# W product and scaling two tiles later, and each rstd broadcast as one transfer to 128 partitions

## The chip, the cores and the metric

The kernel runs on one core of one Trainium2 chip. The metric is device time in microseconds (us): the median over the runs of one kernel.

## The reference

The input x is float32 of shape (2, 64, 256, 256): two images, 64 channels, 65,536 positions each. Four residual steps follow one another:

```python
x = x + conv3x3_depthwise(ln_c(x))                 # layer norm over the 64 channels, eps 1e-6
t = t + scan(batchnorm(ln_t(t) @ W.T), V)          # t: x as tokens; y = sigmoid(wx_t + y @ V.T) along the tokens
x = x + linear_attention(ln_c(x))                  # queries from every position, keys from every 4th row and column
t = t + experts(ln_t(t))                           # 32 experts, each takes its 8 best tokens of the 65,536
```

Each layer norm is (v - mean) / sqrt(var + eps) over the 64 channels of one position. So each position of each image needs one number, rstd = 1 / sqrt(var + eps), and all 64 channels of that position are multiplied by it.

## The kernel before

**Layout.** The 128 partitions hold image times channel: partitions 0 to 63 are the channels of image 0, partitions 64 to 127 those of image 1. The positions lie along the free axis. A tile is 512 positions (128x512, 128 tiles), a block is four tiles (128x2048, 1 MB, 32 blocks). Mean subtraction and the sums over channels are TensorE products with small constant matrices.

**How rstd reaches the channels.** The statistics of a block come out as one rstd number per image and position, on 4 partitions per image (512 positions each). SyncE (SP) writes them to a DRAM scratch, 8 KB per image (`rstd_to_dram`, line 350: one transfer per image, 4 rows of 2 KB). Then it reads each image's row of 2048 numbers back into 64 partitions at once (`rstd_to_channels`, line 359, and line 1313 in the attention stage), which makes a 128x2048 tile that VectorE multiplies with. That is two transfers of 512 KB for each block and norm. For the first norm the tile is `rb[0]`, for the second `rb[1]` (both shown as rstd_wide), for the attention stage `rb3` (rstd_of_channels). Each has two slots, so block k uses slot k % 2.

**The first stage (lines 214 to 635)** computes the first residual step and, behind it, the second norm and the W product. It is a software pipeline written by hand: each engine runs a Python loop over steps t, one tile per step, and each operation of tile g stands at step g + lag. The lags are in one line:

```python
SQ, CENTER, TAPS, SUMS, FINISH, SQ1, PROJECT, SCALE = -4, 5, 8, 9, 10, 12, 20, 21
STATS = (0, 16)
```

In words: ScalarE squares x at g - 4; TensorE sums block n's statistics at step 4n (`stats_of`, for block n of the first norm and block n - 4 of the second in one round n); VectorE forms the variance at 4n + 1 (line 605); ScalarE turns it into rstd at 4n + 2; TensorE centers tile g at g + 5 and VectorE multiplies it by rstd (`norm_x`, line 576); the nine taps of the convolution are shared out between TensorE (line 431), VectorE (line 599) and ScalarE with GpSimd (lines 509 and 541); GpSimd finishes x1 at g + 10 (line 548); TensorE makes the W product at g + 20 (`project`, line 446) and VectorE scales it by the second rstd at g + 21 (`scale_wx`, line 614), into `u`, a ring of two blocks shown as wx. On VectorE, at one step, the order is: first tap, `scale_wx`, second tap, variance, other taps, `norm_x`.

SP is a queue of its own, in program order. For each step t it does, as far as they fall due: the rstd writes of round n at t = 4n + 2, the broadcasts of round n at 4n + 3 (first norm of block n, then second norm of block n - 4), `store_x1` of block k at 4k + 14 (line 366), `store_u` of block k at 4k + SCALE + 4 = 4k + 25 (line 370), and the load of block k of x at 4k - 7 (line 344). Every one stands behind its own semaphore waits, and what stands behind it waits too. A broadcast waits until the rstd writes of its round have landed, and until its slot has been read.

**The attention stage (lines 1203 to 1600)** has the same form with its own lags: statistics at 4k + 10, rstd written at 4k + 12 (line 1304), broadcast at 4k + 13 (line 1313), VectorE's first use at 4k + 16 (`scale_query`, line 1540). Behind a broadcast SP has, for other blocks: the writes of the second rstd of the stage (line 1304), two half-block stores of transposed x (line 1337), the four small broadcasts to the experts (line 1325, 128 KB each), a load (line 1041) and a store of x3 (line 1333).

In between lie the recurrence over the tokens (738 to some 1040 us) and the key and value sums; after the attention stage come the 32 experts and the scatter of their outputs.

Of the kernel before, what the change touches and what calls it, by code (L numbers as in the profile page):

```python
# [15 lines left out]
B, C, H, W = 2, 64, 256, 256  # L16
# [3 lines left out]
BLOCK = 2048  # L20
# [48 lines left out]
def build_program(nc, x, conv_k, ffn_w, ffn_v, gamma, beta, q_w, q_b, kv_w, kv_b, proj_w, proj_b,  # L69
# [4 lines left out]
    with stack:  # L74
        def sb(name, shape, dt=F32, where=stack):
            return where.enter_context(nc.sbuf_tensor(name, shape, dt))
# [4 lines left out]
        def dram(name, shape, dt=F32):  # L81
            return nc.dram_tensor(name, shape, dt, kind="Internal").ap()
# [131 lines left out]
        with ExitStack() as ph:  # L214
# [15 lines left out]
            rb = [sb(f"rstd_wide{l}", [P, 2, BLOCK], F32, ph) for l in range(2)]  # L230
# [14 lines left out]
            rstd_d = [dram(f"rstd_scratch{l}", (NBLK, B, BLOCK)) for l in range(2)]  # L245
# [7 lines left out]
            rb_loaded = [[S(f"rstd_wide{l}_loaded{r}") for r in range(2)] for l in range(2)]  # L253
# [8 lines left out]
            blk = ph.enter_context(nc.Block())  # L262

            SQ, CENTER, TAPS, SUMS, FINISH, SQ1, PROJECT, SCALE = -4, 5, 8, 9, 10, 12, 20, 21
            STATS = (0, 16)
            BEHIND = (STATS[1] - STATS[0]) // TPB
            ROUNDS = NBLK + BEHIND
# [2 lines left out]
            def round_of(l, k):  # L271
                return k + BEHIND * l

            def norms_in(n):

                return [(l, n - BEHIND * l) for l in range(2) if 0 <= n - BEHIND * l < NBLK]

            def rstd_written(n):

                return rstd_out[n % 2], sum(16 * B * len(norms_in(m)) for m in range(n % 2, n + 1, 2))  # L280
# [10 lines left out]
            def block_at(t, lag):  # L291

                k, rest = divmod(t - lag, TPB)
                return k if rest == 0 and 0 <= k < NBLK else None

            def round_at(t, lag):

                n, rest = divmod(t - lag, TPB)
                return n if rest == 0 and 0 <= n < ROUNDS else None
# [4 lines left out]
            def loaded_x(k):  # L304
                return x_loaded[k % SEMS], 16 * (k // SEMS + 1)

            def stored_x1(k):
                return x1_stored[k % SEMS], 16 * (k // SEMS + 1)
# [26 lines left out]
            @blk.sync  # L335
            def _(sp):
                def load(k):
                    r = k % XSLOTS
                    if k >= SEMS:
                        sp.wait_ge(*loaded_x(k - SEMS))  # L340
                    if k >= XSLOTS:
                        sp.wait_ge(wx_ready, TPB * (k - XSLOTS + 1))
                        sp.wait_ge(*stored_x1(k - XSLOTS))
                    sp.dma_start(X[:, r, :], x_v[:, k * BLOCK:(k + 1) * BLOCK]).then_inc(x_loaded[k % SEMS], 16)

                def rstd_to_dram(n):
                    sp.wait_ge(rstd_ready, n + 1)
                    for l, k in norms_in(n):
                        for b in range(B):
                            sp.dma_start(rstd_d[l][k, b, :].rearrange("(j n) -> j n", n=TILE),  # L350
                                         rstd[16 * l + 8 * b:P:32, n % 2, :]).then_inc(rstd_out[n % 2], 16)

                def rstd_to_channels(l, k):
                    if l == 0 or k >= NBLK - BEHIND:
                        sp.wait_ge(*rstd_written(round_of(l, k)))
                    if k >= 2:
                        sp.wait_ge((normed, u_ready)[l], TPB * (k - 1))
                    for b in range(B):
                        sp.dma_start(rb[l][b * C:(b + 1) * C, k % 2, :],
                                     rstd_d[l][k, b, :].partition_broadcast(C)).then_inc(rb_loaded[l][k % 2], 16)  # L360

                def store_x1(k):
                    sp.wait_ge(x1_ready, TPB * (k + 1))
                    if k >= SEMS:
                        sp.wait_ge(*stored_x1(k - SEMS))
                    sp.dma_start(x1_d[k, :, :], X[:, k % XSLOTS, :]).then_inc(x1_stored[k % SEMS], 16)

                def store_u(k):
                    sp.wait_ge(u_ready, TPB * (k + 1))
                    sp.dma_start(xl_d[k, :, :], u[:, k % 2, :]).then_inc(u_stored[k % 2], 16)  # L370

                for t in range(-8, STEPS_A):
                    if (n := round_at(t, 2)) is not None:
                        rstd_to_dram(n)
                    if (n := round_at(t, 3)) is not None:
                        for l, k in norms_in(n):
                            rstd_to_channels(l, k)
                    if (k := block_at(t, FINISH + TPB)) is not None:
                        store_x1(k)
                    if (k := block_at(t, SCALE + TPB)) is not None:  # L380
                        store_u(k)
                    if (k := block_at(t, -7)) is not None:
                        load(k)
                for k in range(NBLK - SEMS, NBLK):
                    sp.wait_ge(*stored_x1(k))
                for r in range(2):
                    sp.wait_ge(u_stored[r], 16 * NBLK // 2)
# [171 lines left out]
            def _(dve):  # L559
                dve.wait_ge(pads_ready, 1)  # L560

                def norm_x(g):
                    k, q = g // TPB, g % RT
                    dve.wait_ge(centered, g + 1)
                    dve.wait_ge(rb_loaded[0][k % 2], 32 * (k // 2 + 1))
                    if g >= RT:
                        done = g - RT + 2
                        dve.wait_ge(taps_ready, done)
                        dve.wait_ge(products, act_taps[done])
                        dve.wait_ge(acc_step, dve_taps[done])  # L570
                    ps, scale = wide(psc[g % 2]), rb[0][:, k % 2, cols_of(g % TPB)].rearrange("p (r w) -> p r w", w=W)
                    if q == 0 and g:
                        dve.tensor_tensor(xn[:, 2 * RT + 1, 1:W + 1], ps[:, 0, :], scale[:, 0, :], ALU.mult).then_inc(halo, 1)
                    if q == RT - 1 and g < NT - 1:
                        dve.tensor_tensor(xn[:, 0, 1:W + 1], ps[:, 1, :], scale[:, 1, :], ALU.mult).then_inc(halo, 1)
                    dve.tensor_tensor(xn[:, 1 + 2 * q:3 + 2 * q, 1:W + 1], ps, scale, ALU.mult).then_inc(normed, 1)  # L576
# [30 lines left out]
                def scale_wx(g):  # L607
                    k = g // TPB
                    dve.wait_ge(wx_ready, g + 1)
                    dve.wait_ge(rb_loaded[1][k % 2], 32 * (k // 2 + 1))  # L610
                    if g % TPB == 0 and k >= 2:
                        dve.wait_ge(u_stored[k % 2], 16 * (k // 2))
                        dve.wait_ge(u_squared, TPB * (k - 1))
                    dve.scalar_tensor_tensor(out=u_steps(g), in0=stepped(psw[g % 2][:, :]), scalar=1.0,  # L614
                                             in1=stepped(rb[1][:, k % 2, cols_of(g % TPB)]), op0=ALU.mult, op1=ALU.mult,
                                             accum_out=sums[:, 0, g:g + 1]).then_inc(u_ready, 1)
# [585 lines left out]
        with ExitStack() as ph:  # L1202
# [5 lines left out]
            rb3 = sb("rstd_of_channels", [P, 2, BLOCK], F32, ph)  # L1208
# [22 lines left out]
            r3_d = dram("rstd3_scratch", (NBLK, B, BLOCK))  # L1231
# [5 lines left out]
            rb3_loaded = [S(f"rstd_of_channels_loaded{r}") for r in range(2)]  # L1237
# [53 lines left out]
            def _(sp):  # L1291
# [15 lines left out]
                def rstd_to_channels(k):  # L1307
                    n = round_of[0, k]
                    sp.wait_ge(rstd_out[n % 2], 32 * (n // 2 + 1))
                    if k >= 2:  # L1310
                        sp.wait_ge(q_scaled, TPB * (k - 1))
                    for b in range(B):
                        sp.dma_start(rb3[b * C:(b + 1) * C, k % 2, :],
                                     r3_d[k, b, :].partition_broadcast(C)).then_inc(rb3_loaded[k % 2], 16)

                def rstd_to_experts(k):

# [208 lines left out]
            def _(dve):  # L1526
# [6 lines left out]
                def scale_query(g):  # L1533
                    k = g // TPB
                    dve.wait_ge(q_ready, g + 1)
                    dve.wait_ge(rb3_loaded[k % 2], 32 * (k // 2 + 1))
                    if g >= QRING:
                        dve.wait_ge(expq_ready, g - QRING + 1)
                        dve.wait_ge(mapped, g - QRING + 1)
                    dve.tensor_tensor(qs[:, g % QRING, :], pq[g % 2][:, :], rb3[:, k % 2, cols_of(g % TPB)], ALU.mult).then_inc(q_scaled, 1)  # L1540
# [426 lines left out]
```

## Time and profile before

| | us |
|---|---|
| median of 3 runs | 1866.84 |
| lowest and highest run | 1864.80 and 1868.62 |
| the profiled execution: its device time | 1866.96 |
| the profiled execution: its span, first to last instruction | 1865.2 |

| engine | busy, us | share of the span |
|---|---|---|
| TensorE (PE), matmul | 1439.8 | 77% |
| VectorE (DVE) | 1384.8 | 74% |
| ScalarE (ACT) | 1218.7 | 65% |
| GpSimd (POOL) | 1398.2 | 75% |

### The profile page before, as it was taken

The numbers are of one execution on the slowest core, as the hardware profiler recorded it, in microseconds if no ns is written. First come the engines' busy times: TensorE is split into PE (matmuls) and PEld (weight loads), VectorE is DVE, ScalarE is ACT, GpSimd is POOL, SyncE is SP. The second block draws the span as 40 slices with busy tenths as digits, with TensorE's granted clock in tenths as the row PEclk, the third lists the DMA queues.
The fourth block names the chain that finished last, engine by engine and source line by source line (L and its number), as shares of the span: only waits on it lengthen the run. The fifth ranks groups of instructions, "written<-read, shape, count | busy, mean of one in ns | idle before, by whom it ended". The sixth has DMA issues, their size and how long they took to land. (4 is left out here: it accounts for less than half of the span.)

```text
span 1865.2 us, 23730 instructions
## 1 busy us (share of the span) xinstructions
PE 1439.8 (77%) x5369; PEld 588.6 (32%) x5369; DVE 1384.8 (74%) x2395; ACT 1218.7 (65%) x2321; POOL 1398.2 (75%) x1029
## 2 busy tenths in 40 slices
PE   3888888888888883799981879999999999925200
PEld 1233333333333321366650523333333333204200
DVE  1888898989988992599974548999999999961000
ACT  2767777777777764599971468888898889620000
POOL 2988888888888890078879049999999999901476
PEclk8999999999999997899995889999999999965555
DMA  4588878888888765959995437888988888561011
GB/s 150 160 233 250 267 242 258 252 262 250 259 249 257 211 203 183 404 231 420 423 390 240 167 92 241 290 272 278 294 287 281 274 287 251 189 174 40 2 2 2
DMA packets 111403, 429.77 MB, mean 230 GB/s; under 512 B 44672, under 2 KB 47648, under 8 KB 66208
## 3 DMA queue, kind: packets, MB, share of 16 engines
q1 hardware_dynamic: 91376, 423.77, 69.5%
q10 hardware_dynamic: 16432, 4.29, 1.4%
q8 instruction: 47, 0.77, 0.2%
q0 software_dynamic: 3456, 0.19, 0.2%
q14 instruction: 92, 0.75, 0.1%
HBM read 257.89 MB, written 170.01 MB: 229 GB/s over the span
## 5 line engine op out<-in xcount | busy, mean ns | idle before, releaser
L599 DVE SCALAR_TENSOR_TENSOR pst<-xn,kk,pst 128x512 f32<-128x512 f32 x448 | 336.1, 750 | 8.2 <-PE pst L431 2.0
L431 PE MATMUL pst<-xn,taps 128*128 128x512 f32 x512 | 250.4, 612 | 89.6 <-DVE acc L599 89.6
L541 POOL TENSOR_TENSOR x_and_products<-tap_products,x_and_products 128x512 f32<-128x512 f32 x192 | 245.3, 1278 | 29.9 <-ACT tap_products L509 2.5
L1508 POOL TENSOR_SCALAR exp_q<-exp_q 128x512 f32<-128x512 f32 x128 | 189.7, 1482 | 73.1 <-ACT exp_q L1459 73.1
L925 DVE SCALAR_TENSOR_TENSOR pss<-region,bn,pss 128x256 f32<-128x256 f32 x432 | 195.7, 489 | 45.4 <-PE pss L837 44.9
L509 ACT ACTIVATE tap_products<-xn,kk 128x512 f32<-128x512 f32 x320 | 212.7, 709 | 13.6 <-POOL x_and_products L541 9.0
L548 POOL TENSOR_TENSOR x_ring<-acc,x_and_products 128x512 f32<-128x512 f32 x128 | 163.9, 1280 | 66.5 <-DVE acc L599 65.2
L1503 POOL TENSOR_TENSOR sq_norm<-x_ring 128x512 f32<-128x512 f32 x128 | 188.9, 1476 | 5.7 <-DVE x_ring L1555 2.3
L541 POOL TENSOR_TENSOR x_and_products<-tap_products,x_ring 128x512 f32<-128x512 f32 x128 | 163.5, 1278 | 19.8 <-ACT tap_products L509 19.8
L874 POOL TENSOR_TENSOR x_block<-x_block,region 128x2048 f32<-128x2048 f32 x28 | 155.6, 5558 | 20.2 <-DMA x_block<-x_scratch 16.7
L431 PEld LDWEIGHTS pst<-xn,taps 128*128 128x128 f32 x512 | 92.4, 191 | 234.8 <-issue 234.6
L1515 POOL TENSOR_TENSOR q_z<-q_map,z_inv 128x512 f32<-128x512 f32 x128 | 164.5, 1285 | 0.0
L471 ACT ACTIVATE sq<-x_ring 128x512 f32<-128x512 f32 x256 | 146.4, 616 | 7.1 <-DMA x_ring<-in_x 3.7
L446 PE MATMUL psw<-x_ring,wcT 128*128 128x512 f32 x256 | 135.3, 615 | 15.3 <-DVE wx L614 15.2
L614 DVE SCALAR_TENSOR_TENSOR wx<-psw,rstd_wide 128x512 f32<-128x512 f32 x128 | 87.5, 684 | 77.5 <-issue 54.8
L1392 PE MATMUL ps_denominator<-q_map,dT 128*128 128x512 f32 x256 | 138.2, 621 | 8.7 <-DVE q_map L1549 7.3
L1386 PE MATMUL ps_query<-x_ring,qcT 128*128 128x512 f32 x256 | 140.3, 632 | 3.8 <-DVE query L1540 3.8
L837 PE MATMUL pss<-region,vT 128*128 128x256 f32 x480 | 126.7, 388 | 18.2 <-ACT region L866 17.8
L1775 POOL DMA_INDIRECT out<-fin,word_of_slot x88 | 86.7, 985 | 71.6 <-DVE fin L1929 45.1
L440 PE MATMUL psc<-x_ring,cst 128*128 128x512 f32 x256 | 136.7, 617 | 3.6 <-DVE xn L576 3.6
L1465 ACT ACTIVATE ln_d<-ps_denominator,cols 128x512 f32<-128x512 f32 x128 | 86.9, 679 | 72.5 <-PE ps_denominator L1392 72.3
L1398 PE MATMUL ps_attended<-q_z,mT 128*128 128x512 f32 x256 | 131.8, 597 | 1.1 <-POOL q_z L1515 1.1
(237 smaller groups left out, 2867.9 us busy)
## 6 DMA issues: line engine op xcount, KB each, us to landing
rstd_wide<-rstd_scratch SPq DMA_DIRECT2D x128, 512.0 KB, 7.9
x_ring<-in_x SPq DMA_DIRECT2D x32, 1024.0 KB, 10.7
x_scratch<-x_ring SPq DMA_DIRECT2D x32, 1024.0 KB, 4.3
xl_scratch<-wx SPq DMA_DIRECT2D x32, 1024.0 KB, 8.7
region<-xl_scratch SPq DMA_DIRECT2D x32, 1024.0 KB, 12.6
x_ring<-x_scratch SPq DMA_DIRECT2D x32, 1024.0 KB, 5.2
rstd_of_channels<-rstd_scratch SPq DMA_DIRECT2D x64, 512.0 KB, 7.7
out<-x_ring SPq DMA_DIRECT2D x32, 1024.0 KB, 6.6
```

The source lines that it names most:

```text
L431: m = pe.matmul(wide(pst[g % 2]), taps[:, n * P:(n + 1) * P], tap_rows(g, t), start=(n == 0), stop=(n == len(mine) - 1))
L471: act.activation(sq[l][:, g % TPB, :], x_tile(g), ACT.Square).then_inc(squared[l], 1)
L509: act.activation(prod[:, q % NP, :, :], tap_rows(g, t), ACT.Copy, scale=kk[:, t:t + 1]).then_inc(products, 1)
L541: pool.tensor_tensor(xr[:, g % XR, :], prod[:, q % NP, :, :].rearrange("p r w -> p (r w)"), xr[:, g % XR, :] if n else x_tile(g), ALU.add) ...
L548: pool.tensor_tensor(x_tile(g), acc[:, g % 2, :, :].rearrange("p r w -> p (r w)"), xr[:, g % XR, :], ALU.add).then_inc(x1_ready, 1)
L599: dve.scalar_tensor_tensor(out=out, in0=tap_rows(g, t), scalar=kk[:, t:t + 1], in1=wide(pst[g % 2]), op0=ALU.mult, op1=ALU.add).then_inc(a ...
L874: pool.tensor_tensor(in_chunks(x1_x2), in_chunks(x1_x2), y, ALU.add).then_inc(added, 1)
L925: dve.scalar_tensor_tensor(out=ps_at(r, j), in0=u, scalar=gain_w, in1=ps_at(r, j), op0=ALU.mult, op1=ALU.add).then_inc(summed, 1)
L1386: pe.matmul(pq[g % 2][:, :], qcT[:, :], x_tile(g), start=True, stop=True).then_inc(q_ready, 1)
L1503: pool.tensor_tensor(sq[1][:, g % SQSLOTS[1], :], x_tile(g), x_tile(g), ALU.mult).then_inc(squared[1], 1)
L1508: pool.tensor_scalar(e, e, 1.0, None, ALU.min).then_inc(clipped, 1)
L1515: pool.tensor_tensor(qz[:, g % 2, :], qm[:, g % QSLOTS, :], zr[:, g % 2, :], ALU.mult).then_inc(qz_ready, 1)
```

## The change

The lags PROJECT and SCALE grow from 20 and 21 to 22 and 23. With SCALE, the store of u moves from 4k + 25 to 4k + 27, the step of the broadcasts, behind which it then stands. The load of x moves from 4k - 7 to 4k - 6, the step of the rstd writes and of `store_x1`, behind which it then stands and ahead of the broadcasts. Each broadcast of rstd is issued as one transfer of 1 MB: its source has the counts 2 (images), 64 (channels, step 0) and 2048 (positions), its target the 128 partitions. The waits on it count 16 in place of 32 for each use.

```diff
-            SQ, CENTER, TAPS, SUMS, FINISH, SQ1, PROJECT, SCALE = -4, 5, 8, 9, 10, 12, 20, 21
+            SQ, CENTER, TAPS, SUMS, FINISH, SQ1, PROJECT, SCALE = -4, 5, 8, 9, 10, 12, 22, 23
...
-                    for b in range(B):
-                        sp.dma_start(rb[l][b * C:(b + 1) * C, k % 2, :],
-                                     rstd_d[l][k, b, :].partition_broadcast(C)).then_inc(rb_loaded[l][k % 2], 16)
+                    sp.dma_start(rb[l][:, k % 2, :],
+                                 rstd_d[l][k, :, :].unsqueeze(1).to_broadcast([B, C, BLOCK])).then_inc(rb_loaded[l][k % 2], 16)
...
-                    if (k := block_at(t, -7)) is not None:
+                    if (k := block_at(t, -6)) is not None:
                         load(k)
...
-                    dve.wait_ge(rb_loaded[0][k % 2], 32 * (k // 2 + 1))
+                    dve.wait_ge(rb_loaded[0][k % 2], 16 * (k // 2 + 1))
...
-                    dve.wait_ge(rb_loaded[1][k % 2], 32 * (k // 2 + 1))
+                    dve.wait_ge(rb_loaded[1][k % 2], 16 * (k // 2 + 1))
...
-                    for b in range(B):
-                        sp.dma_start(rb3[b * C:(b + 1) * C, k % 2, :],
-                                     r3_d[k, b, :].partition_broadcast(C)).then_inc(rb3_loaded[k % 2], 16)
+                    sp.dma_start(rb3[:, k % 2, :],
+                                 r3_d[k, :, :].unsqueeze(1).to_broadcast([B, C, BLOCK])).then_inc(rb3_loaded[k % 2], 16)
...
-                    dve.wait_ge(rb3_loaded[k % 2], 32 * (k // 2 + 1))
+                    dve.wait_ge(rb3_loaded[k % 2], 16 * (k // 2 + 1))
```

## Rows read from the trace of the kernel before

**Rows 1.** The page: the span, and each engine's busy time, share, instructions.

```profile
span 1865.2 us, 23730 instructions
...
PE 1439.8 (77%) x5369; PEld 588.6 (32%) x5369; DVE 1384.8 (74%) x2395; ACT 1218.7 (65%) x2321; POOL 1398.2 (75%) x1029
```

**Rows 2.** Windows: length; PE, PEld, DVE, ACT, POOL busy; clock, DMA share, GB/s.

```profile
100.00:600.00 500.00, 433.71 (x1535) 162.61 (x1534) 444.99 (x768) 367.22 (x716) 424.56 (x338) 0.99 0.84 252
...
1100.00:1600.00 500.00, 495.10 (x1870) 161.72 (x1867) 461.24 (x686) 436.96 (x762) 495.63 (x357) 1.00 0.84 267
```

**Rows 3.** Line 614 between 100 and 690 us: idle before it (us, times).

```profile
  issue: 47.1, 25
```

**Rows 4.** Timeline of DVE: start, us, instruction, idle before it in brackets.

```profile
418.18 0.69 DVE L614 SCALAR_TENSOR_TENSOR wx<-psw,rstd_wide 128x512 f32<-128x512 f32 x1 [1.53 <-issue]
...
421.50 0.68 DVE L576 TENSOR_TENSOR xn<-psc,rstd_wide 128x512 f32<-128x512 f32 x1
```

**Rows 5.** Timeline of SP's queue, one block of the first stage.

```profile
401.79 2.12 SPq L350 DMA_DIRECT2D rstd_scratch<-rstd  x4
404.02 0.39 SPq L366 DMA_DIRECT2D x_scratch<-x_ring  x1
405.12 3.04 SPq L359 DMA_DIRECT2D rstd_wide<-rstd_scratch  x4
412.38 0.34 SPq L370 DMA_DIRECT2D xl_scratch<-wx  x1
412.83 0.37 SPq L344 DMA_DIRECT2D x_ring<-in_x  x1
```

**Rows 6.** DMA issues: count, KB each, median us from issue to landing.

```profile
rstd_wide<-rstd_scratch SPq DMA_DIRECT2D x128, 512.0 KB, 7.9
x_ring<-in_x SPq DMA_DIRECT2D x32, 1024.0 KB, 10.7
...
rstd_of_channels<-rstd_scratch SPq DMA_DIRECT2D x64, 512.0 KB, 7.7
```

**Rows 7.** Windows: a stretch of broadcasts alone, and one of plain copies alone.

```profile
409.50:416.80 7.30, 7.30 (x41) 2.59 (x34) 7.01 (x12) 5.53 (x11) 6.92 (x6) 1.00 1.01 215
...
750.00:780.00 30.00, 21.35 (x56) 9.51 (x56) 13.21 (x27) 13.20 (x28) 0.00 (x0) 0.85 1.01 423
```

**Rows 8.** DMA view from 32.5 to 35.4 us: two rstd writes alone.

```profile
DMA packets 16, 0.02 MB, mean 6 GB/s; under 512 B 8, under 2 KB 8, under 8 KB 16
...
rstd_scratch<-rstd SPq DMA_DIRECT2D x2, 8.0 KB
```

**Rows 9.** DMA view from 35 to 45 us: packets and their sizes.

```profile
DMA packets 320, 2.11 MB, mean 211 GB/s; under 512 B 56, under 2 KB 56, under 8 KB 64
```

**Rows 10.** Timeline of SP's queue in the attention stage.

```profile
1302.26 1.73 SPq L1325 DMA_DIRECT2D xsub<-rstd_scratch  x4
1304.23 0.35 SPq L1041 DMA_DIRECT2D x_ring<-x_scratch  x1
1305.20 1.34 SPq L1304 DMA_DIRECT2D rstd_scratch<-rstd  x2
...
1309.36 1.85 SPq L1313 DMA_DIRECT2D rstd_of_channels<-rstd_scratch  x2
```

**Rows 11.** Timeline of DVE: the last broadcast's use, and the next stage's start.

```profile
728.74 0.69 DVE L614 SCALAR_TENSOR_TENSOR wx<-psw,rstd_wide 128x512 f32<-128x512 f32 x1 [7.70 <-issue]
...
738.49 0.42 DVE L647 TENSOR_REDUCE bn<-sums 128x2 f32<-128x256 f32 x1 [4.42 <-PEq L214]
```

**Rows 12.** SP's queue: first broadcast of the run; first and last of the attention stage.

```profile
34.59 1.12 SPq L359 DMA_DIRECT2D rstd_wide<-rstd_scratch  x2
...
1085.64 1.12 SPq L1313 DMA_DIRECT2D rstd_of_channels<-rstd_scratch  x2
...
1593.31 2.18 SPq L1313 DMA_DIRECT2D rstd_of_channels<-rstd_scratch  x2
```

## The prediction, made before the run

> **What bounds the kernel now.** The page first: in a span of 1865.2 us VectorE is busy for 74% and GpSimd for 75% [rows 1], so no engine bounds the whole, and the stages are read one by one. In the windows [rows 2] the attention stage shows GpSimd at 495.6 of 500 us: there the engine is the bound, and the DMA engines still have room (share 0.84). The first stage has no such engine: VectorE 445.0, TensorE 433.7 and GpSimd 424.6 of 500 us. Its missing tenth is found by asking one line what ended its idle time: `scale_wx`, line 614, waits 47.1 us in 25 places between 100 and 690 us [rows 3], once in nearly every block. In one block it looks so [rows 4, 5]: rstd is written from 401.79 us, the four broadcasts are issued from 405.12 us, and `scale_wx` starts at 418.18 us after 1.53 us of idling, while `norm_x`, which uses the broadcast issued first, follows at 421.50 us without a wait. "issue" as releaser means that the profile names nobody; the broadcast's landing, a median of 7.9 us after its issue [rows 6], is the only other thing line 614 waits for at a block's first tile. Since the next variance stands behind `scale_wx` in VectorE's order, this wait closes a loop: variance, rstd, write, broadcast, `scale_wx`, variance.
>
> One more thing is to be seen in the DMA rows. During broadcasts alone sixteen engines move 215 GB/s, during plain copies 423 GB/s, both at a share of 1.01 [rows 7]. So one engine moves 423 / 16 = 26.4 GB/s of plain data, and 13.4 GB/s when all sixteen read one 8 KB row over and over.
>
> **The change part by part.**
>
> *W product and scaling two tiles later.* A block takes 20.43 us, a tile 5.1 us. `scale_wx` gets some 10 us more for a broadcast that is 1.53 us late [rows 4]. By itself this removes up to 47.1 us [rows 3]; two more steps at the end of the stage, in which only the W product and its scaling are left, cost about 3 us by the stage's end [rows 11]: four tiles and the change of stage take 738.49 - 728.74 = 9.8 us.
>
> *The load of x and the store of u* move on SP's queue. The load is now issued behind `store_x1` and ahead of the broadcasts, the store of u behind the broadcasts. The load of [rows 5] at 412.83 us would be issued at the next rstd write, about 422 + 3 us; ScalarE's first square of that block stands three steps behind, so the load is 2 steps ahead in place of 3, against 10.7 us to landing [rows 6]. I cost it at nothing: 1 MB at 423 GB/s is 2.5 us, and it fills the time in which SP waits for the rstd write. If that cover went, it would put 2.5 us per block before the broadcasts.
>
> *One transfer in place of two.* This decides. SP saves half of the issues (3.04 us for four, [rows 5]), which nothing waits for. The bytes stay. What may change is on how many DMA engines they run. The trace shows how a transfer is split: two rstd writes alone are 16 packets, 8 of them under 512 B [rows 8], that is, each write's four 2 KB rows are followed by four small packets. Over 10 us with two more writes, two broadcasts of 64 rows and one load of 128 rows there are 320 packets [rows 9]: 8 of 2 KB, 256 of 8 KB, and 56 small ones, which are 2 x 4 + 3 x 16. I read a small packet as one engine reporting its share as done. Then a transfer is cut along its outermost count, and the number of engines follows that count: sixteen for 64 and 128, four for 4. The removed source counted 64 outermost. The new one counts 2 outermost (images), each read 64 times, against 128 on the target's side. No transfer in this trace has a 2 there, so the cost is bounded from both sides: all sixteen engines (the cost of now, or less, as two rows are read at once), or two engines, one per image. I take two, because the nearest row is the four-row write, which is on four engines (four packets could not use more, so the row binds weakly). The Trainium skill ("DMA: Bandwidth & Descriptors", section "Why a DMA increments its semaphore by 16 and not by 1") speaks against this change: it says that a transfer runs on the largest number of engines up to 16 that divides the slowest count of both sides, and, for SP's queue, on the lowest-numbered ones. By that rule 2 and 128 give two engines, always the same two; the four-row writes agree, and nothing yet shows a count of 2.
>
> The price on two engines: 512 KB per engine at 26.4 GB/s is 19.9 us (the plain rate, since two engines ask for 53 GB/s together where sixteen got 215). The program names no engines, so I let all broadcasts take the same two; they queue there behind these engines' sixteenths of the plain copies (64 KB, 2.5 us each).
>
> First stage, per block: two broadcasts 39.7, load, `store_x1`, `store_u` 7.4, rstd writes about 0.4: 47.5 us against 20.43. No wait of another engine is longer, since rstd of the next round is ready while the second broadcast still runs, and load and store fill the 2 to 3 us until a write has landed. In all: 64 broadcasts x 19.86 = 1271; 93 plain copies after the first broadcast x 2.48 = 231; writes 10; together 1512. From the first broadcast at 34.6 us [rows 12], with 1.5 us at either end, and 9.8 us from the last broadcast's landing to the next stage [rows 11]: 34.6 + 1.5 + 1512 + 1.5 + 9.8 = 1559 in place of 738.5, **+821 us**. The two-tile lag is inside this time, and what it gains is lost.
>
> Attention stage, per block: broadcast 19.9, load and store of x3 5.0, two half-block stores 2.6, the experts' 512 KB and the writes 2.0: 29.5 us of queue. Here gaps are added, since SP takes turns [rows 10]: the second rstd's write lands only behind the broadcast, then four small broadcasts are issued (1.7 us), then the load, the next rstd write, and only when that has landed the next broadcast (1302.26 to 1309.36 us now). I add 3 us: 32.6 us, where a block now takes (1593.31 - 1085.64) / 31 = 16.4 [rows 12]. 32 x 16.2 = **+518 us**. Bounds: 29.5 (+419) and 36 (+627).
>
> Sum against the profiled execution: its span 1865.2 plus 1.8 outside is 1866.96, and the median of the runs is 1866.84, so both bases agree. 1867 + 821 + 518 = **3206 us**.
>
> **The rivals.**
>
> *All sixteen engines carry the transfer, and the kernel gets faster.* The place is the wait of line 614. It decides if the split goes by the target's 128 partitions. For it: 128 rows ran on sixteen engines [rows 9]; two rows read at once could even raise the 215 GB/s [rows 7]. Against it: the source's count of 2. Price: 47.1 us of waiting, some 45 of it gained since GpSimd (424.6 of 500) is next [rows 2], less 3 at the end: 1825 us.
>
> *All sixteen carry it, but the wait comes back elsewhere.* The load ahead of the broadcasts makes the one for `norm_x` late; 2.5 us per block is the price, 1.5 us the gain. DMA is at 0.84 [rows 2], which speaks for little room; `norm_x` now stands 3.3 us behind the late one without waiting [rows 4], which speaks against it. About 1867 us.
>
> *Two engines, each at the slow rate.* If re-reading one row is slow by itself and not by sharing it among sixteen, a broadcast takes 512 KB / 13.4 GB/s = 39 us: first stage 64 x 39 + 241 + 47 = 2784 (+2046), attention stage 39 + 9.6 + 3 = 51.6 per block (+1126), 5039 us. Against it: two readers ask for far less than the 215 GB/s which the rows gave.
>
> *Two engines, but other ones for each transfer.* Then the first stage's block holds 19.9 + 7.8 = 27.7 us, +233 in all: 2618 us. The four-row writes say nothing on which engines are taken.
>
> **How the numbers follow.** Two engines at the plain rate: 0.80. Sixteen and faster: 0.13. Sixteen and no change: 0.03. Slow rate: 0.02. Other engines: 0.02. The forecast is the first, 3206 us. Its range: down to the queue alone in the attention stage (3107) and some 150 less should the two engines run faster alone; up to 36 us per block there and 5 us of gap per block in the first stage (160): 3475, and a little for the tails. I give 2950 to 3550, which leaves out the other cases, 0.20 together. A measurement of this kernel can tell about 0.2% from no change; faster 0.13, same 0.03, slower 0.84.
>
> **What would show it.** Right: line 359's 32 + 32 transfers of 1 MB land 20 us or more after issue, mostly 20 to 45; small packets per broadcast are 2 in place of 16; the DMA share falls to some 0.3 in the first stage while its span grows to about 1560 us; `norm_x` and `scale_wx` wait for rstd_wide in every block; blocks are 47 us apart there and some 33 us in the attention stage; line 1540 waits for rstd_of_channels each block; the recurrence between keeps its length. Wrong: a landing near 8 us for 1 MB, with 16 small packets, means sixteen engines, and then line 614's waits tell between the first two rivals; a landing near 40 us for a lone broadcast means the slow rate.

## The result, and the profile after

The changed kernel takes 3205.89 us (median of 4 runs, 3204.97 to 3207.17), the kernel before 1866.24 us: a ratio of 1.7177, 95% interval 1.7147 to 1.7206. The profiled execution has a span of 3204.2 us. The page's head, its busy line and its packet line:

```profile
span 3204.2 us, 23634 instructions
...
PE 1693.6 (53%) x5369; PEld 660.5 (21%) x5369; DVE 1374.5 (43%) x2395; ACT 1232.1 (38%) x2321; POOL 1397.0 (44%) x1029
...
DMA packets 108523, 429.76 MB, mean 134 GB/s; under 512 B 41792, under 2 KB 44768, under 8 KB 63328
```

The engines do the same work as before: VectorE is busy for 1374.5 us against 1384.8 and GpSimd for 1397.0 against 1398.2 [rows 1]. For both of them the 1339 us are idle time. Only TensorE is busy for longer, 1693.6 us against 1439.8 with the same 5369 products: its granted clock between 100 and 600 us was 0.73 (next fence; a mean of its two levels, 1.2 and 2.4 GHz) where it had been 0.99 [rows 2]. It is no bound all the same, since it is busy for only 254.90 of these 500 us. The bytes moved are the same too. What differs are the packets under 512 B: 44,672 on the page of before, 41,792 here, 2880 fewer. The 192 broadcasts of before had 16 each, 3072; 96 merged ones with 2 each are 192; the difference is 2880, to the packet. So each merged transfer ran on two engines, if a small packet is one engine's report, as the prediction reads it; the DMA share below bears that out.

Windows of the changed kernel, with the columns of [rows 2] (the last three are TensorE's clock, the DMA share and GB/s): 500 us of the first stage, 15 us in which nothing but broadcasts is under way, 5 us in which plain copies meet them, and the attention stage.

```profile
100.00:600.00 500.00, 254.90 (x702) 88.79 (x700) 204.08 (x339) 171.31 (x320) 201.87 (x161) 0.73 0.29 105
832.00:847.00 15.00, 8.93 (x19) 3.41 (x17) 6.29 (x11) 9.56 (x20) 10.66 (x9) 0.84 0.13 52
855.00:860.00 5.00, 3.40 (x4) 1.51 (x5) 2.68 (x4) 0.90 (x3) 3.26 (x3) 0.50 1.01 264
2100.00:2900.00 800.00, 493.56 (x1632) 157.98 (x1632) 398.71 (x616) 386.62 (x664) 426.03 (x307) 0.79 0.41 151
```

The second line is the finding in one row: a DMA share of 0.13 is two engines of sixteen, and they move 52 GB/s, 26 each, the plain rate of one engine [rows 7]. Both broadcasts of the round had been issued at 826.17 us (the fence of SP's queue below), and still only two engines are at work. That both sit on the same two shows in the rstd writes, which run on four engines. SP issues four writes from 847.61 us on, 16 packets of 2 KB in all. The DMA lines of 850 to 854 us and of 871.5 to 876 us show when they ran; the packets of 2 KB are the last count less the one before it:

```profile
DMA packets 120, 0.75 MB, mean 186 GB/s; under 512 B 23, under 2 KB 23, under 8 KB 31
...
DMA packets 48, 0.25 MB, mean 55 GB/s; under 512 B 12, under 2 KB 12, under 8 KB 20
```

Eight of the packets run at once, the other eight only 20 us later, just before the next broadcasts at 875.87 us. So two of the four engines of the writes were held by the broadcasts, in this round. SP's queue over one block of the first stage, to be held against [rows 5]:

```profile
798.88 3.06 SPq L350 DMA_DIRECT2D rstd_scratch<-rstd  x3
802.03 0.49 SPq L365 DMA_DIRECT2D x_scratch<-x_ring  x1
802.63 1.14 SPq L344 DMA_DIRECT2D x_ring<-in_x  x1
826.17 1.44 SPq L358 DMA_DIRECT2D rstd_wide<-rstd_scratch  x2
827.66 19.91 SPq L369 DMA_DIRECT2D xl_scratch<-wx  x1
847.61 4.64 SPq L350 DMA_DIRECT2D rstd_scratch<-rstd  x4
852.35 0.38 SPq L365 DMA_DIRECT2D x_scratch<-x_ring  x1
852.84 1.86 SPq L344 DMA_DIRECT2D x_ring<-in_x  x1
875.87 1.11 SPq L358 DMA_DIRECT2D rstd_wide<-rstd_scratch  x2
```

The order is that of the code, but between the rstd writes and the broadcasts there are now over 20 us: the writes use engines on which the broadcasts of the round before are still queued. SP waits for them (us in total, times, longest):

```profile
SPq L358 <- DMA rstd_scratch<-rstd: 680.5, 36, 22.9
```

In the kernel before, the same wait was 27.6 us in all. On VectorE it looks so in one block:

```profile
851.13 0.42 DVE L572 TENSOR_TENSOR xn<-psc,rstd_wide 128x256 f32<-128x256 f32 x1 [12.77 <-DMA rstd_wide<-rstd_scratch]
...
875.32 0.69 DVE L613 SCALAR_TENSOR_TENSOR wx<-psw,rstd_wide 128x512 f32<-128x512 f32 x1 [17.60 <-DMA xl_scratch<-wx]
```

Two waits per block: `norm_x` for the first broadcast, then `scale_wx`. For the second one the profile names the store of u, not the broadcast: at a block's first tile line 613 also waits until its slot of the ring u has been stored. This store lands last of what the line waits for, since it is queued behind the second broadcast. The stages, by the start of the step that follows the first stage and by the attention stage's broadcasts:

```profile
L646 DVE TENSOR_REDUCE bn<-sums x1: 419/419/419, 1625.3 to 1625.3; 128x2 f32<-128x256 f32 x1
```

```profile
L1311 SPq DMA_DIRECT2D rstd_of_channels<-rstd_scratch x32: 527/550/555, 1973.4 to 2922.1; - x32
```

The first stage ends at 1625.3 us, 886.8 later than before [rows 11]. From there to the first broadcast of the attention stage it is 348.1 us, and it was 347.2 in the kernel before [rows 11, 12]: the recurrence is untouched. The rest, some 451 us, is the attention stage's.

### The profile page after: what moved, and what is told of

Same layout as the page of the kernel before. It is cut to its first block and busy times, and to the rows that moved or that the text cites. A ratio compares the mean times of both kernels' runs of the same rounds, so it can differ in the third digit from the quotient of the medians.

```text
span 3204.2 us, 23634 instructions
## 1 busy us (share of the span) xinstructions
PE 1693.6 (53%) x5369; PEld 660.5 (21%) x5369; DVE 1374.5 (43%) x2395; ACT 1232.1 (38%) x2321; POOL 1397.0 (44%) x1029
## 2 busy tenths in 40 slices
DMA packets 108523, 429.76 MB, mean 134 GB/s; under 512 B 41792, under 2 KB 44768, under 8 KB 63328
## 5 line engine op out<-in xcount | busy, mean ns | idle before, releaser
L430 PE MATMUL pst<-xn,taps 128*128 128x512 f32 x512 | 352.1, 825 | 423.8 <-DVE acc L598 423.8
L1384 PE MATMUL ps_query<-x_ring,qcT 128*128 128x512 f32 x256 | 172.0, 761 | 382.2 <-DVE query L1538 382.2
L439 PE MATMUL psc<-x_ring,cst 128*128 128x512 f32 x256 | 170.0, 753 | 335.7 <-DVE xn L575 335.7
L1538 DVE TENSOR_TENSOR query<-ps_query,rstd_of_channels 128x512 f32<-128x512 f32 x128 | 86.9, 680 | 451.0 <-issue 429.1
L1457 ACT ACTIVATE exp_q<-query,cols 128x512 f32<-128x512 f32 x128 | 91.4, 714 | 426.7 <-DVE query L1538 426.7
L430 PEld LDWEIGHTS pst<-xn,taps 128*128 128x128 f32 x512 | 119.2, 251 | 631.5 <-issue 629.5
L445 PE MATMUL psw<-x_ring,wcT 128*128 128x512 f32 x256 | 167.9, 750 | 60.6 <-DVE wx L613 58.5
L575 DVE TENSOR_TENSOR xn<-psc,rstd_wide 128x512 f32<-128x512 f32 x128 | 87.6, 685 | 229.4 <-DMA rstd_wide<-rstd_scratch 224.3
L1390 PE MATMUL ps_denominator<-q_map,dT 128*128 128x512 f32 x256 | 167.9, 743 | 7.6 <-DVE q_map L1547 7.4
L1384 PEld LDWEIGHTS ps_query<-x_ring,qcT 128*128 128x128 f32 x256 | 54.7, 238 | 478.4 <-issue 477.4
```

The source lines that it names most:

```text
L430: m = pe.matmul(wide(pst[g % 2]), taps[:, n * P:(n + 1) * P], tap_rows(g, t), start=(n == 0), stop=(n == len(mine) - 1))
L439: pe.matmul(psc[g % 2][:, :], center, x_tile(g), start=True, stop=True).then_inc(centered, 1)
L445: pe.matmul(by_step(psw[g % 2][:, :]), wcT[:, :], in_chunks(x_tile(g)), start=True, stop=True).then_inc(wx_ready, 1)
L1384: pe.matmul(pq[g % 2][:, :], qcT[:, :], x_tile(g), start=True, stop=True).then_inc(q_ready, 1)
L1390: pe.matmul(pd[:, :], dT[:, :], qm[:, g % QSLOTS, :], start=True, stop=True).then_inc(d_ready, 1)
```

## The experiments

Theory: the outermost count of the transfer sets the number of DMA engines, and the queue of two engines sets the time. Rivals: the moved lags and load are part of the loss; one large transfer with a repeated source is slow by itself. In all kernels everything is computed. Ratios are to the kernel before.

**The lags alone.** Both broadcasts again two transfers of 64 rows, lags and load as changed.

```diff
-                    sp.dma_start(rb[l][:, k % 2, :],
-                                 rstd_d[l][k, :, :].unsqueeze(1).to_broadcast([B, C, BLOCK])).then_inc(rb_loaded[l][k % 2], 16)
+                    for b in range(B):
+                        sp.dma_start(rb[l][b * C:(b + 1) * C, k % 2, :],
+                                     rstd_d[l][k, b, :].partition_broadcast(C)).then_inc(rb_loaded[l][k % 2], 16)
...
```

> The lags 22 and 23 and the moved load alone; each broadcast again as two transfers of 64 rows. Theory (two engines carry the merged transfer, the lags cost nothing): 1825 us, as in the rival of the prediction; a block of the first stage falls from 20.4 to about 19 us and line 614's 47.1 us of waiting between 100 and 690 us go to nearly nothing. Rival (the moved lags and the moved load are part of the slowdown): over 1900 us. Third possibility: 1860 to 1870 us, the wait comes back at norm_x.

Measured: 1810.18 us, ratio 0.9691 (0.9669 to 0.9712). The first stage ends at 683.1 us, 55.4 earlier than before. The same window as in [rows 2]:

```profile
100.00:600.00 500.00, 470.80 (x1692) 181.42 (x1685) 490.43 (x846) 407.97 (x787) 470.49 (x375) 1.00 0.96 276
```

VectorE went from 445.0 to 490.4 of 500 us: it is the bound now. Between 100 and 690 us line 614 no longer waits for a broadcast or for "issue" at all. What is left of its idle time (us, times):

```profile
  DMA xl_scratch<-wx: 11.5, 2
  PE psw L446: 9.6, 6
```

The lags are a gain, not a loss. The DMA share rose from 0.84 to 0.96.

**The merged transfer alone,** with the lags and the load of before.

```diff
-            SQ, CENTER, TAPS, SUMS, FINISH, SQ1, PROJECT, SCALE = -4, 5, 8, 9, 10, 12, 22, 23
+            SQ, CENTER, TAPS, SUMS, FINISH, SQ1, PROJECT, SCALE = -4, 5, 8, 9, 10, 12, 20, 21
...
-                    if (k := block_at(t, -6)) is not None:
+                    if (k := block_at(t, -7)) is not None:
```

> The merged transfer alone, with the lags and the load of before. Theory (two engines): 3200 us within 60, the period of a block is the queue of the two engines, 47 to 49 us in the first stage and about 31 in the attention stage, whatever the lags. Rival (the lags set the loss): near 1867 us or clearly below 3200.

Measured: 3318.09 us (one run), 112 us above the changed kernel and outside the 3200 us within 60 that were expected. The loss comes from the merged transfer, "whatever the lags" is wrong. The reason stands in one line of VectorE's timeline:

```profile
815.75 0.69 DVE L613 SCALAR_TENSOR_TENSOR wx<-psw,rstd_wide 128x512 f32<-128x512 f32 x1 [34.14 <-DMA rstd_wide<-rstd_scratch]
```

With the old lag the tile that needs the second broadcast is scaled in the step of the next variance and ahead of it. The next rstd, and the next round's broadcasts, wait for it, and the two engines run dry in the meantime: SP issues the next writes at 819.80 us and the broadcasts at 823.12 us, and the DMA share is 0.04 until then.

```profile
819.60:823.00 3.40, 3.40 (x5) 1.33 (x5) 3.33 (x7) 3.40 (x7) 3.26 (x3) 0.50 0.04 12
```

With the new lags the scaling comes two steps later, behind the variance. The first stage ends at 1731.3 us, 106.0 later than with the new lags. The load of x was moved along with the lags here; its own part in the 106 us was not tried.

**Two copies of rstd,** so that the source counts 4 outermost (eight copies: the same with 8, and 16 outermost).

```diff
-            rstd_d = [dram(f"rstd_scratch{l}", (NBLK, B, BLOCK)) for l in range(2)]
+            COPIES = 2
+            rstd_d = [dram(f"rstd_scratch{l}", (NBLK, B * COPIES, BLOCK)) for l in range(2)]
...
-                            sp.dma_start(rstd_d[l][k, b, :].rearrange("(j n) -> j n", n=TILE),
-                                         rstd[16 * l + 8 * b:P:32, n % 2, :]).then_inc(rstd_out[n % 2], 16)
+                            sp.dma_start(rstd_d[l][k, b * COPIES:(b + 1) * COPIES, :].rearrange("r (j n) -> j r n", n=TILE),
+                                         rstd[16 * l + 8 * b:P:32, n % 2, :].unsqueeze(1)
+                                         .to_broadcast([TPB, COPIES, TILE])).then_inc(rstd_out[n % 2], 16)
...
-                                 rstd_d[l][k, :, :].unsqueeze(1).to_broadcast([B, C, BLOCK])).then_inc(rb_loaded[l][k % 2], 16)
+                                 rstd_d[l][k, :, :].unsqueeze(1).to_broadcast([B * COPIES, C // COPIES, BLOCK])).then_inc(rb_loaded[l][k % 2], 16)
...
```

> As the changed kernel, but rstd is written twice per image to the scratch, so that the one transfer's source counts 4 outermost (4 rows, each read 32 times) against 128 partitions. Theory (the outermost count sets the engines): four engines, 9.9 us per broadcast, a block of the first stage 19.9 + 7.4 + 0.7 = 28 us, of the attention stage 9.9 + 9.6 + 2 = 21.5 us; in all 1867 + 32 x 7.6 + 32 x 5.1 = 2273 us; 4 small packets per broadcast. Rival (a single transfer of 1 MB with a repeated source is slow by itself, however many rows it has): about 3200 us. Second rival (sixteen engines as soon as the source is cut in any other way): 1830 to 1870 us.

Measured: 2467.68 us (one run), between the two rivals. The packet line, and a window of broadcasts alone:

```profile
DMA packets 109483, 431.33 MB, mean 175 GB/s; under 512 B 41984, under 2 KB 44960, under 8 KB 64288
```

```profile
401.00:407.00 6.00, 5.10 (x13) 2.00 (x11) 3.54 (x7) 4.90 (x10) 5.60 (x5) 1.00 0.26 108
```

41,984 are 192 more small packets than in the changed kernel: two more for each of 96 broadcasts, four in all. The DMA share is 0.26, four of sixteen, at twice the 52 GB/s. The time missed 2273 us by 195: the expectation had 28 us for a block of the first stage and 21.5 for the attention stage, where tile to tile 29.0 and 25.0 were measured (`norm_x` from 57.4 to 977.9 us, `scale_query` from 1426.6 to 2220.0 us, each 127 tiles), and nothing for the rounds with one broadcast at the stage's two ends. The number of engines came as expected; the sum was too short, and why the attention stage takes 3.5 us more per block is open.

**Eight copies.** 16 outermost.

> As the changed kernel, but rstd is written eight times per image, so that the one transfer's source counts 16 outermost (16 rows, each read 8 times). Theory (outermost count): sixteen engines, and each engine now reads a row of its own, so a broadcast goes at the plain rate, 1 MB in 2.5 us of queue in place of 4.8; landing in 5 us or less; the first stage is bound by its engines, 1825 us or less, at or below the kernel with the lags alone. Rival (a repeated read is slow by itself, 215 GB/s whatever row): 1825 to 1870 us, with 4.8 us of queue per broadcast.

Measured: 1908.41 us, ratio 1.0214 (1.0187 to 1.0241). 43,137 small packets: 1345 more than in the changed kernel, which is 14 for each of 96 broadcasts, and one. So sixteen engines, as the count says, and 1297 us less than with a count of 2 in the same single transfer. But it is 98 us behind the lags alone, and a window of broadcasts shows no plain rate:

```profile
411.00:415.50 4.50, 4.50 (x12) 1.87 (x10) 1.72 (x3) 3.72 (x8) 1.60 (x2) 1.00 1.00 229
```

229 GB/s with a row for each engine, against 215 with one row for all [rows 7]. Both expectations on the time failed, though the rival's rate was nearly right. Two more kernels take the 98 us apart.

**Eight copies written, one read.** Lags as changed, the writes of the kernel with eight copies, two transfers of 64 rows that read one copy. The cut below is against the kernel with eight copies.

```diff
-                    sp.dma_start(rb[l][:, k % 2, :],
-                                 rstd_d[l][k, :, :].unsqueeze(1).to_broadcast([B * COPIES, C // COPIES, BLOCK])).then_inc(rb_loaded[l][k % 2], 16)
+                    for b in range(B):
+                        sp.dma_start(rb[l][b * C:(b + 1) * C, k % 2, :],
+                                     rstd_d[l][k, b * COPIES, :].partition_broadcast(C)).then_inc(rb_loaded[l][k % 2], 16)
...
```

> The kernel with the lags alone, with rstd written eight times, as in the kernel with eight copies, and only one copy read, in two transfers of 64 rows. It tells why eight copies took 1908 us where the lags alone take 1810. Theory (the writes are to blame: 128 packets of 2 KB on the same four engines for each round, and the broadcast waits for them): above 1870 us. Rival (the reads are to blame: a small source read many times is slow even when each engine has a row of its own): 1815 us or less.

Measured: 1922.00 us, ratio 1.0296 (1.0266 to 1.0326). The writes are to blame: they alone put 112 us on the 1810 us. SP's wait for them in the first stage, in this kernel, is 83.7 us, where the lags alone have 34.4:

```profile
SPq L361 <- DMA rstd_scratch<-rstd: 83.7, 36, 6.0
```

These are 49 us more, while the first stage ends 82.5 us later than with the lags alone (765.6 against 683.1 us). How the rest of the loss comes about is not shown.

**Eight copies apart.** The 16 rows 256 KB apart.

```diff
-            rstd_d = [dram(f"rstd_scratch{l}", (NBLK, B * COPIES, BLOCK)) for l in range(2)]
+            rstd_d = [dram(f"rstd_scratch{l}", (B * COPIES, NBLK, BLOCK)) for l in range(2)]
...
```

> As the kernel with eight copies, but the 16 rows lie 256 KB apart in DRAM in place of 8 KB. Theory of the small source (128 KB within few places of the memory limits the reads): the 8 KB packets of a broadcast take 0.31 us in place of 0.55 to 0.9, and the time falls below 1908 us, at most to 1815 us if the writes cost nothing. Rival (repeated reads are slow wherever the rows lie, or the writes are to blame): 1900 us or more.

Measured: 1911.44 us, ratio 1.0238 (1.0208 to 1.0267), no different from 8 KB apart. A window of its broadcasts:

```profile
411.00:416.00 5.00, 5.00 (x13) 2.16 (x12) 2.91 (x6) 3.92 (x8) 2.46 (x2) 1.00 1.02 241
```

241 GB/s. That sixteen engines re-reading rows get little over half the plain rate is neither due to their sharing a row nor to the rows lying close.

**The merged transfer in the attention stage alone.** The lags alone, with line 1311 of the changed kernel.

> The kernel with the lags alone, and the merged transfer in the attention stage only. Theory (each stage pays its own queue of two engines): 1810 + 451 = 2261 us, where 451 is what the attention stage took longer in the changed kernel; 30.6 us from broadcast to broadcast there, the first stage as with the lags alone. Rival (the loss of one stage is made by the other, by a queue left over): clearly less or more than 451.

Measured: 2274.11 us (one run), 464 above the lags alone where 451 were expected. Its broadcasts there run from 1027.0 to 1990.0 us, 31.1 us apart, and the first stage ends at 683.0 us as with the lags alone. The stages pay separately: the first stage of the changed kernel ends 942.2 us later than with the lags alone (1625.3 against 683.1 us), 464 + 942 = 1406, and both together cost 3205.9 - 1810.2 = 1396 us. So the losses add up to within some 10 us.

**The load of x where it was.** The lags alone, with the load at 4k - 7.

```diff
-                    if (k := block_at(t, -6)) is not None:
+                    if (k := block_at(t, -7)) is not None:
```

> The kernel with the lags alone, but the load of x again at 4k - 7. Theory (the gain is the later use of the second broadcast): 1810 us within 4. Rival (the earlier load of x is part of the gain): 1820 to 1850 us, with ScalarE's squares waiting for x_ring.

Measured: 1805.72 us, ratio 0.9672 (0.9657 to 0.9687), which overlaps the interval of the lags alone. The load's place is worth nothing that can be told, and the gain is the lags'. Both kernels beat the one before and the changed one.

## Why the prediction was right, and where its steps were not

**What bounds the kernel now: right.** The loop through line 614's wait was the first stage's bound. With the lags alone the wait is gone, and VectorE is busy for 98% of the window. One sentence was too narrow: the broadcast is not the only other thing that line 614 waits for at a block's first tile. It also waits for its slot of u, and that wait is the one that the profile names in the changed kernel.

**The lags: right in direction, sized too small, and wrongly called lost.** The rival without the two-engine queue gave 1825 us; 1810 were measured. The term that was too small is the wait: [rows 3] holds only what is named "issue" and only between 100 and 690 us. Over the whole stage line 614 of the kernel before stood idle for 77.5 us (us, times):

```profile
  issue: 54.8, 26
  DMA rstd_wide<-rstd_scratch: 15.7, 3
  PE psw L446: 7.0, 6
```

With the lags alone it is 11.5 + 9.6 = 21.1 us, 56.4 less, and the stage ends 55.4 us earlier. And "what it gains is lost" was false: inside the slow kernel the lags, with the load's new place, still save 112 us, because they take the second broadcast out of the way of the next variance.

**The load and the store of u at nothing: right** for the load (1805.72 against 1810.18 us, without the merged transfer). The store of u was not tried alone. In the changed kernel its issue stops SP for some 20 us, and the rstd writes stand behind it. But the two engines are not out of work for it. This is the DMA share from 800 to 895 us in tenths, 40 slices; two busy engines of sixteen are a 1, and no slice falls below it:

```profile
DMA  1899211111111111111183799411111111111111
```

So what bounds these rounds is the work of the two engines, and the order in which it is queued costs little there.

**One transfer in place of two: right, and this decides.** Two engines (2880 small packets fewer), the same two for both broadcasts of a round (share 0.13 with both queued, and half of the rstd writes held up), each at 26 GB/s. The row that the choice rested on, four rows on four engines, was weak, as the prediction said; counts of 4 and 16 on the same transfer, with 4 and 16 small packets, now carry it. The Trainium skill ("DMA: Bandwidth & Descriptors", section "Why a DMA increments its semaphore by 16 and not by 1") gives 2, 4 and 16 engines for these three sources, and the traces agree with each.

**The two sums: each off by about 65 us, with opposite signs.** The total of 3206 us was met to the microsecond only because they cancel, which is luck.

- First stage, +821 predicted, +886.8 measured. From the broadcasts of the fifth round to those of the last full one a block took 49.3 us, not 47.5:

```profile
134.69 1.11 SPq L358 DMA_DIRECT2D rstd_wide<-rstd_scratch  x2
...
1466.53 1.10 SPq L358 DMA_DIRECT2D rstd_wide<-rstd_scratch  x2
```

  (1466.53 - 134.69) / 27 = 49.3; over 28 blocks that is 50 of the 66 us. The step that failed is the price of the packets beside plain copies: 2.5 us per copy was taken from copies alone, but where load and stores meet a broadcast all sixteen engines are busy (share 1.01) and move 264 GB/s, not 423. Over the 5 us of that window this is an estimated 5 x (1 - 264 / 423) = 1.9 us, about the 1.8 us that a block took longer. The remaining 16 us lie outside these rounds, at the stage's two ends; how they come about is open.
- Attention stage, +518 predicted, some +451 measured. From broadcast to broadcast it is (2922.1 - 1973.4) / 31 = 30.6 us, not 32.6: the gap in which the two engines run dry was put at 3 us above 29.5 of queue and is about 1, if the 29.5 us hold, which were not measured by themselves. SP's queue there, to be held against [rows 10]:

```profile
2510.15 1.74 SPq L1323 DMA_DIRECT2D xsub<-rstd_scratch  x4
2512.06 1.40 SPq L1040 DMA_DIRECT2D x_ring<-x_scratch  x1
2513.50 1.03 SPq L1303 DMA_DIRECT2D rstd_scratch<-rstd  x2
...
2518.62 0.56 SPq L1311 DMA_DIRECT2D rstd_of_channels<-rstd_scratch  x1
...
2542.58 1.74 SPq L1323 DMA_DIRECT2D xsub<-rstd_scratch  x4
```

  From the experts' broadcasts to the next large one it takes 8.5 us (2510.15 to 2518.62), in which the two engines have the four small broadcasts, a load, two stores and the writes to do; little of it is idle.

**The rivals.** Sixteen engines: ruled out by the packets. The slow rate of 13.4 GB/s per engine: ruled out by the 52 GB/s of two. Other engines for each transfer: ruled out by the share of 0.13 with two broadcasts queued, and by 3206 us where that rival has 2618.

## What to carry to other kernels

With 128 partitions on the target's side, the number of DMA engines followed here from the outermost count of the source (2, 4 and 16 engines for 2, 4 and 16 rows), not from the bytes, 1 MB each time. So before two transfers are merged into one, look at what stands outermost in the new access pattern, and count the small packets of the trace afterwards. A change of two parts should be taken apart: here the lags were worth 3% (1810 us against 1867), and the merged transfer, which cost 77% on top of them (3206 against 1810), hid it. And a total that is met to the microsecond proves nothing about its terms; the stages have to be held against their own rows.

## What the runs showed that was not expected

- SP's issue of a transfer can stop. In the changed kernel the store of u, right behind two broadcasts with 64 packets each on two engines, took 19.91 us to issue (0.34 us in [rows 5]). With 64 such packets queued on an engine instead of 128 the issues behind a broadcast are short: with two copies, the store of u takes a median of 0.46 us. What is full then was not tried.
- Sixteen engines that read rows repeatedly get 215 to 241 GB/s, whether they share one 8 KB row, have rows of their own 8 KB apart, or 256 KB apart; two and four engines on the same kind of source get 52 and 108 GB/s, the plain rate. Why is open.
- Writing rstd eight times, some 11 MB more in the whole run, costs 112 us, though the two stages move hundreds of MB. Each write still has four small packets, so it goes to four engines only, and the next broadcast waits for it; that this is the whole of the 112 us is not shown.
